# Layer 0 start and first expert tiles: where loads, statistics, products of ones and tile turns stand

## The chip, the cores and the metric

The kernel runs on one core of one Trainium2 chip. The metric is the device time of one execution in microseconds; lower is better. The kernel before took 1592.35 us, the median of three runs (1588.64, 1592.35 and 1593.25 us).

## What is computed

Two layers over 4096 tokens of width 256 (8 sequences of 512 in layer 0, 4 of 1024 for the recurrence of layer 1). Both add attention and a mixture of experts to the residual, from one layer norm:

```python
x = L0_attn_in_features
xn = _layernorm(x, axis=-1)
x = x + _L0_attn_ref(xn, ...) + _L0_ffn_ref(xn, ...)
xn = _layernorm(x, axis=-1)
x = x + _L1_attn_ref(xn, ...) + _L1_ffn_ref(xn, ...)
```

`_L0_attn_ref` is causal attention with 16 heads of 16. `_L0_ffn_ref` routes each token to 2 of 8 experts of width 512 and adds a shared network:

```python
h = _gelu(jnp.einsum('td,edf->tef', xt, Wu))
y = jnp.einsum('tef,efd->ted', h, Wd)
moe = jnp.einsum('ted,te->td', y, cw)
shared = _gelu(xt @ W1) @ W2
```

Layer 1 has a gated linear recurrence (8 heads of 32) and 8 experts of width 1024, again 2 for each token. The change touches layer 0 alone.

## The kernel before

Each engine has its own stream of instructions, written in one function for each (`sync` for SP, which issues nearly all DMAs, `gpsimd` for POOL, `scalar` for ACT, `tensor` for PE, `vector` for DVE). They meet through semaphores. The order of the attention stage is one list of steps, `attention_order()`; each engine walks it and does its part of each step. So moving a step in the list moves it on every engine that takes part in it.

A block is 512 tokens, with `x_load(b)` as its load of 512 KB. Its statistics are made by DVE for blocks 0 to 3 and by ACT for blocks 4 to 7 (`stats0`, eight passes over 256 elements). `xt` turns the normalised block with eight transposes on PE, `project(n, m)` makes queries (m = 0) or keys (m = 1) for eight heads, group n. These are cut into three bfloat16 parts: ACT takes the first, DVE the remainder and the second, POOL the third (`low_part`). SP stores the parts to DRAM (`split_out`) and, when both stores of a group are there, reads them back in another layout (`stack(n)`, 12 DMAs), from which `scores` and `scoresT` multiply. `scores` is made for the row maxima alone; the maxima go to the stacks through `maxrow(n)` (a DMA of SP), and `scoresT(n, j)` waits for them. Its exponentials are ACT's. Before the main loop a prelude handles blocks 0 and 1 and stacks 0 and 1; `ln0_steps()` spreads the normalisation of the others over the first positions of the loop.

SP's order at the start: constants, `x_load(0)`, Wq, Wk, `x_load(1)`, Wg, Wv, `x_load(2)`, `x_load(3)`; behind the store of normalised block 0 the `late_loads` (blocks 4 to 7 and Wo in four pieces); behind the 12 DMAs of `stack(0)` FW1 and the two halves of FW2, the first copies of the shared network's weights, which serve block 0 (`first_up`, `first_gelu`, `first_down`, lines 1605 and 1614) before the transposed scores begin.

At the end of layer 0's attention PE makes the shared products of blocks 1 and 2 (`HB` is 3: later blocks have theirs in the next layer), `shared_down(b, i)` with 8 matmuls each (line 1674). DVE adds their results in pairs (`shared_add`, counted by `sh_added`). Then come the experts: sorted tokens lie in 71 tiles of 128. POOL gathers a tile's rows (line 1005). For the first 8 tiles of a layer PE turns them in bank 0 of PSUM (`tile_turn`, line 1685) and DVE copies them out (line 2251). DVE also copies the expert's up weights (`weights`, line 2277). `expert_up(0, i)` writes bank 1 or 2 (line 1700), ACT takes the Gelu (line 1294), `expert_down` multiplies with Wd (line 1718). The shared products lie in banks 2 and 3. Wu and Wd (4 MB each) are loaded by SP once the attention is over; DVE waits for Wu in front of its first weights (`wu_in`), PE for Wd in front of its first down products, on line 1712. Where an expert's number is read into a register, that is a load of the engine's sequencer.

## Time and profile before

| | us |
|---|---|
| median of three runs | 1592.35 |
| profiled execution | 1598.56 |
| its span, first to last instruction | 1596.8 |
| PE busy | 1514.8 (95%) |
| DVE, ACT, POOL busy | 847.8, 746.2, 706.3 |

The profile is of one execution. Line numbers are those of the kernel before, and times on a timeline count from the span's start. PE is TensorE, PEld its weight loads, DVE VectorE, ACT ScalarE, POOL GpSimd, SP SyncE; a q behind a name is the engine's queue or sequencer. A time in brackets is idle time of the engine before the instruction, with what ended it. The clock column is the clock of TensorE that was granted, as a share of full speed (2.4 GHz; 0.50 is 1.2 GHz).

### The profile page before, as it was taken

To read this page: it belongs to the slowest core of one execution; us is meant where nothing else is said; L and a number is where in the kernel's file an instruction comes from. 1 tells how busy PE (TensorE), PEld (TensorE's weight loads), DVE (VectorE), ACT (ScalarE), POOL (GpSimd) and SP (SyncE) were. 2 spreads that over 40 slices of the span, in tenths; PEclk is the share of its full clock that TensorE was granted. 3 is DMA by queue.
4 is the path that set the end of the run, shared out by engine and by line. 5 is a ranking of instruction groups with operands and counts; after the bars stand their busy time and mean duration, and the time that the engine had idled before them with its cause. 6 is when DMAs were issued, how large, how long until landed. Compare 5 with 4: busy or idle time off the path is not lost.

```text
span 1596.8 us, 32512 instructions
## 1 busy us (share of the span) xinstructions
PE 1514.8 (95%) x10874; PEld 1168.8 (73%) x10874; DVE 847.8 (53%) x2400; ACT 746.2 (47%) x1953; POOL 706.3 (44%) x815
## 2 busy tenths in 40 slices
PE   5988989999999999999987899999999999999997
PEld 3455545555548999997664577769999999999996
DVE  4777898888713444442577988874232222223230
ACT  4665655555641323323566676545333343343432
POOL 3232326667623555553710388852333433333331
PEclk9999999999999999999998999999999999999999
DMA  8534344555215444435621489647333333333331
GB/s 266 142 114 118 98 98 83 110 111 86 68 70 201 110 114 116 111 112 147 187 94 56 123 190 177 123 79 267 56 55 54 48 59 54 57 57 54 60 54 21
DMA packets 155835, 167.60 MB, mean 105 GB/s; under 512 B 84992, under 2 KB 132988, under 8 KB 153628
## 3 DMA queue, kind: packets, MB, share of 16 engines
q1 hardware_dynamic: 131132, 128.15, 32.8%
q0 software_dynamic: 24544, 37.38, 11.0%
q8 instruction: 94, 1.54, 0.4%
q14 instruction: 65, 0.53, 0.2%
HBM read 104.10 MB, written 44.45 MB: 93 GB/s over the span
## 4 chain that ended last, share of the span: by engine, by line
PE 81%; DVE 8%; ACT 3%; issue 3%; DMA 3%; SPq 1%; POOL 0%; DVEq 0%; another core or an unknown queue 0%; ACTq 0%; POOLq 0%
PE PS L1700 23%; PE PS L1718 23%; PE PS L1557 4%; PE PS L1521 3%; PE PS L1542 3%; PE PS L1811 3%; PE PS L1493 3%; PE PS L1674 2%; DVE PS L2023 2%; PE PS L1628 2%; PE PS L1823 2%; PE PS L1583 2%; PE PS L1909 1%; PE PS L1503 1%; ACT arena L1216 1%
## 5 line engine op out<-in xcount | busy, mean ns | idle before, releaser
L1700 PEld LDWEIGHTS PS<-arena 128*128 128x128 f32 x3408 | 396.6, 192 | 11.4
L1700 PE MATMUL PS<-arena 128*128 128x128 f32 x3408 | 403.1, 275 | 0.0
L1718 PE MATMUL PS<-arena 128*128 x1704 | 392.4, 379 | 0.8 <-ACT arena L1294 0.8
L1718 PEld LDWEIGHTS PS<-arena 128*128 128x128 f32 x1704 | 311.9, 190 | 41.1 <-issue 1.2
L2023 DVE CUSTOM_DVE_ANT_0 PS<-PS,arena 128x512 f32<-128x512 f32 (+3 forms) x512 | 235.5, 523 | 48.1 <-PE PS L1521 45.1
L1019 POOL DMA_INDIRECT out<-arena x71 | 111.6, 1571 | 299.4 <-ACT arena L1312 277.6
L1302 ACT ACTIVATE arena<-PS,arena 128x128 f32<-128x128 f32 x568 | 162.3, 369 | 134.6 <-PE PS L1700 132.9
L2276 DVE COPY arena<-arena 128x8 f32 x71 | 12.4, 174 | 353.3 <-ACT arena L1302 334.7
L1312 ACT ACTIVATE arena<-PS,arena 128x256 f32<-128x256 f32 x142 | 67.4, 475 | 256.8 <-PE PS L1720 177.6
L1005 POOL DMA_INDIRECT arena<-XN,arena x142 | 144.0, 1014 | 91.9 <-issue 38.4
L1216 ACT ACTIVATE arena<-PS 128x512 f32<-128x512 f32 (+1 forms) x256 | 166.0, 704 | 32.6 <-PE PS L1542 29.2
L952 POOL TENSOR_SCALAR_AFFINE_SELECT arena<-arena 128x256 f32<-128x256 f32 x256 | 98.4, 409 | 183.2 <-ACT arena L1216 182.0
L2277 DVE COPY arena<-arena 128x1024 f32 (+1 forms) x142 | 136.4, 961 | 73.0 <-ACT arena L1294 57.5
L978 POOL DMA_INDIRECT SLOT<-arena x128 | 156.6, 1223 | 28.5 <-issue 28.2
L1012 POOL DMA_INDIRECT SUM<-arena x71 | 70.6, 994 | 96.4 <-ACT arena L1312 96.4
L1521 PE MATMUL PS<-arena 96*128 96x512 bf16 (+3 forms) x512 | 100.8, 306 | 8.8 <-DVE arena L2023 6.8
L1542 PE MATMUL PS<-arena 99*128 99x512 bf16 (+3 forms) x512 | 96.4, 302 | 7.1 <-ACT arena L1216 5.9
L1294 ACT ACTIVATE arena<-PS 128x512 f32<-128x512 f32 x71 | 42.4, 598 | 113.6 <-issue 73.9
L1542 PEld LDWEIGHTS PS<-arena 99*128 99x128 bf16 x512 | 44.4, 98 | 57.7 <-issue 17.2
L1521 PEld LDWEIGHTS PS<-arena 96*128 96x128 bf16 x512 | 48.4, 98 | 51.5 <-DVE arena L2023 16.9
L2265 DVE COPY arena<-arena 128x512 uint16<-128x512 uint16 x126 | 53.9, 428 | 60.0 <-DMA arena<-XN,arena 57.9
L1557 PE MATMUL PS<-arena 128*32 128x512 f32 (+3 forms) x1024 | 75.7, 435 | 0.5 <-issue 0.4
(248 smaller groups left out, 1993.9 us busy)
## 6 DMA issues: line engine op xcount, KB each, us to landing
arena<-FD SPq DMA_DIRECT2D x32, 512.0 KB
SPL<-arena SPq DMA_DIRECT2D x32, 384.0 KB, 3.4
arena<-SPL SPq DMA_DIRECT2D x64, 192.0 KB
XN<-arena SPq DMA_DIRECT2D x16, 512.0 KB, 3.2
arena<-SPL SPq DMA_DIRECT2D x64, 128.0 KB
arena<-SUM SPq DMA_DIRECT2D x16, 512.0 KB, 6.4
arena<-in_w SPq DMA_DIRECT2D x16, 512.0 KB
arena<-in_w SPq DMA_DIRECT2D x8, 1024.0 KB
```

The costliest lines, as they stand in the source:

```text
L978: pool.indirect_dma_start(SLOT[layer], bass.IndirectOffsetOnAxis(ap=POS[:, n, i:i + 1], axis=0), META[:, i, n, :], None).then_inc(row_out[ ...
L1005: pool.indirect_dma_start(MOE[layer].xr[i % 4][:, :], None, XN, row).then_inc(tile_in[i % 4], 16)
L1019: pool.indirect_dma_start(out, row, m.y[i % 3][:, :], None, compute_op=ALU.add).then_inc(y_out[i % 3], 16)
L1216: act.activation(PB[h % NPB][:, lo:hi], ps(3, lo, hi), ACT.Exp, scale=0.25).then_inc(p_made)
L1302: ins = act.activation(m.hT[i % len(m.hT)][:, 128 * f:128 * f + 128], ps(m.UPB[i % 2], 128 * f, 128 * f + 128), ACT.Gelu, bias=m.bias[i % ...
L1521: ins = pe.matmul(ps(0, o, o + w), q[0:96, j, 128 * i:128 * i + 128], k[0:96, j, 0:w], start=True, stop=True)
L1542: ins = pe.matmul(ps(3, o, o + w), k[0:99, j, 128 * kb:128 * kb + 128], q[0:99, j, 128 * kb:512], start=True, stop=True)
L1557: ins = pe.matmul(PS[32 * j:32 * j + 32, 6, 128 * kb:512], vb[:, kb, 8 * half + jj, :], PB[(8 * n + jj) % NPB][:, OFFT[kb]:OFFT[kb] + w], ...
L1700: ins = pe.matmul(o, m.now[i % 2][:, c * F + 128 * f:c * F + 128 * f + 128], m.xt[i % 2][:, 128 * c:128 * c + 128], start=(c == 0), stop=( ...
L1718: ins = pe.matmul(to, m.hT[i % len(m.hT)][:, 128 * c:128 * c + 128], m.WD[:, bass.ds(e * (nf * 256) + c * 256, 256)], start=(c == 0), stop ...
L2023: dve.tensor_tensor_reduce(sc, sc, MASK[:, 384 - 128 * r:512], -1.0, -NEG, ALU.add, ALU.min, NM[n % 2][:, r, j:j + 1]).then_inc(s_max)
L2277: dve.tensor_copy(m.now[i % 2][:, :], m.WU[:, bass.ds(e * m.wrow, m.wrow)]).then_inc(w_staged)
```

## The change

It has five parts, all in layer 0. (1) PE waits for the first constant and then makes 42 products of ones with ones in an unused bank, ahead of the first transposes. (2) Behind the store of normalised block 0 SP loads block 4 only. Blocks 5 to 7, FW1 and FW2 in halves and Wo follow behind `stack(0)`, in mixed order. (3) The statistics of block 5 move from the end of the prelude to the second position of the loop. (4) The semaphore of Wv and Wo is split: Wv counts with Wg, Wo has its own, and the counts of the shared weights' semaphore follow. (5) The turns of expert tiles 0 and 1 go between the last four shared down products, on PE and in DVE's order; the wait for the last shared addition moves from the front of the experts to the products of tile 1, which write a bank that the shared products use.

```diff
 def ln0_steps():
     yield []
-    yield []
+    yield [("stats", 5)]
...
-    out += [..., ("logits", 1), ("logitsT", 1), ("stats", 5)]
+    out += [..., ("logits", 1), ("logitsT", 1)]
...
-            sp.dma_start(WV[:, :, :], t["Wv"]).then_inc(wvo_in, 16)
+            sp.dma_start(WV[:, :, :], t["Wv"]).then_inc(wr_in, 16)
...
             def late_loads():
-                for b in range(4, NB):
-                    x_load(b)
+                x_load(5)
+                for k in range(2):
+                    sp.dma_start(FW1[:, k, :], t["W1"][:, k, :]).then_inc(w12_in, 16)
+                x_load(6)
+                for k in range(2):
+                    sp.dma_start(FW2[k], t["W2"][:, 2 * k:2 * k + 2, :]).then_inc(w12_in, 16)
+                x_load(7)
                 heads = t["Wo"].rearrange("(j r) g n -> j r g n", r=32)
                 for g in range(4):
                     lo = 64 * (g % 2)
-                    sp.dma_start(WO[lo:lo + 64, g // 2, :], heads[:, 0:16, g, :]).then_inc(wvo_in, 16)
+                    sp.dma_start(WO[lo:lo + 64, g // 2, :], heads[:, 0:16, g, :]).then_inc(wo_in, 16)
...
                 if kind == "norm" and a[0] < 2:
                     norm0(*a)
                     if a[0] == 0:
-                        late_loads()
+                        x_load(4)
...
                     stack(*a)
                     if a[0] == 0:
-                        sp.dma_start(FW1[:, :, :], t["W1"]).then_inc(w12_in, 16)
-                        for k in range(2):
-                            sp.dma_start(FW2[k], t["W2"][:, 2 * k:2 * k + 2, :]).then_inc(w12_in, 16)
+                        late_loads()
...
+            def spin(bk, o, many):
+                for _ in range(many):
+                    pe.matmul(ps(bk, o, o + 128), ones[:, :], ones[:, :], start=True, stop=True)
+
             def xt(b, c):
+                if b == 0 and c == 0:
+                    pe.wait_ge(const_set, 1)
+                    spin(3, 0, 42)
                 pe.wait_ge(*normed0(b))
...
             def logits(b):
                 xnt_ready(b)
-                pe.wait_ge(wr_in, 16)
+                pe.wait_ge(wr_in, 32)
...
             def project_v(b, half):
                 xnt_ready(b)
-                pe.wait_ge(wvo_in, 80)
+                pe.wait_ge(wr_in, 32)
...
             def output(b, half):
+                if b == 0:
+                    pe.wait_ge(wo_in, 64)
...
             def first_up(fc):
-                pe.wait_ge(w12_in, 48)
+                pe.wait_ge(w12_in, 64)
...
             def expert_up(layer, i):
                 pe.wait_ge(w_staged, NTILE * layer + i + 1)
+                if i == 1 and layer == 0:
+                    pe.wait_ge(sh_added, 4 * HB)
...
             def experts(layer):
                 m = MOE[layer]
-                tile_turn(layer, 0)
-                tile_turn(layer, 1)
+                if layer:
+                    tile_turn(layer, 0)
+                    tile_turn(layer, 1)
...
-            for i in range(4):
-                shared_down(HB - 1, i)
+            shared_down(HB - 1, 0)
+            tile_turn(0, 0)
+            shared_down(HB - 1, 1)
+            shared_down(HB - 1, 2)
+            tile_turn(0, 1)
+            shared_down(HB - 1, 3)
...
-            pe.wait_ge(sh_added, 4 * HB)
+            pe.wait_ge(sh_added, 4 * HB - 2)
             experts(0)
...
                 dve.wait_ge(b1_put, 1)
+                if layer == 0:
+                    dve.wait_ge(sh_gelu, 4 * HB - 4)
                 for i in range(2):
                     weights(layer, i)
                     tile_turn(layer, i)
+                    if layer == 0:
+                        shared_add(HB - 1, i)
...
-            for b in range(1, HB):
-                for half in range(2):
-                    shared_add(b, half)
-            dve.wait_ge(sh_gelu, 4 * HB - 4)
+            for half in range(2):
+                shared_add(1, half)
             experts(0)
```

## Rows read from the trace of the kernel before

**Rows 1.** The page: the chain that ended last, by engine.

```profile
PE 81%; DVE 8%; ACT 3%; issue 3%; DMA 3%; SPq 1%; POOL 0%; DVEq 0%; another core or an unknown queue 0%; ACTq 0%; POOLq 0%
```

**Rows 2.** Timeline of PE, first 75 us: start, duration, line, operation [idle before <-releaser].

```profile
12.00 1.97 PE L1464 MATMUL PS<-arena 128*128 128x128 f32 x8 [12.00 <-DVE arena L1977]
...
14.79 9.40 PE L1493 MATMUL PS<-arena 128*128 128x512 f32 x16 [0.83 <-issue]
...
34.45 1.22 PE L1521 MATMUL PS<-arena 96*128 96x512 bf16 x4 [1.74 <-DMA arena<-SPL]
...
67.87 0.72 PE L1542 MATMUL PS<-arena 99*128 99x512 bf16 x4
```

**Rows 3.** Durations (min/median/max ns) of the projections, line 1493, first 50 us.

```profile
L1493 PE MATMUL PS<-arena x24: 590/592/1194, 14.8 to 41.2; 128*128 128x512 f32 x24
```

**Rows 4.** Windows: length, busy PE, PEld, DVE, ACT, POOL, clock, DMA share, GB/s.

```profile
38.00:40.00 2.00, 2.00 (x7) 0.81 (x6) 0.24 (x1) 0.60 (x1) 0.00 (x0) 0.53 1.01 364
...
64.00:66.00 2.00, 2.00 (x14) 1.62 (x14) 1.19 (x7) 0.98 (x2) 0.64 (x1) 1.00 0.20 69
```

**Rows 5.** Timeline of PE, 460 to 512 us.

```profile
475.59 14.03 PE L1674 MATMUL PS<-arena 128*128 128x256 f32 x64
...
492.37 3.74 PE L1700 MATMUL PS<-arena 128*128 128x128 f32 x32
...
497.13 2.00 PE L1718 MATMUL PS<-arena 128*128 x8 [0.81 <-ACT arena L1294]
```

**Rows 6.** Timelines of POOL and DVE, first 50 us.

```profile
0.82 0.21 POOL L924 MEMSET arena<- 128x128 f32 x1 [0.29 <-POOLq L2558]
...
17.00 1.38 DVE L1977 TENSOR_SCALAR arena<-arena 128x256 f32<-128x256 f32 x4
...
22.66 1.09 POOL L956 TENSOR_TENSOR arena<-arena 128x512 bf16<-128x512 f32 x1 [1.05 <-DVE arena L2011]
```

**Rows 7.** Timeline of SP, first 80 us; last, the page's part 6.

```profile
21.64 2.50 SPq L714 DMA_DIRECT2D SPL<-arena  x2
...
28.21 5.56 SPq L729 DMA_DIRECT2D arena<-SPL  x12
...
44.09 5.43 SPq L729 DMA_DIRECT2D arena<-SPL  x12
...
54.74 5.43 SPq L729 DMA_DIRECT2D arena<-SPL  x12
...
61.04 0.85 SPq L738 DMA_DIRECT2D arena<-arena  x1
...
SPL<-arena SPq DMA_DIRECT2D x32, 384.0 KB, 3.4
```

**Rows 8.** Timeline of ACT, 41 to 70 us.

```profile
41.85 0.60 ACT L1189 ACTIVATE arena<-PS 128x512 bf16<-128x512 f32 x1 [2.12 <-PE PS L1493]
...
50.08 0.31 ACT L1138 ACTIVATE arena<-arena 128x16 f32<-128x16 f32 x1
...
56.28 0.60 ACT L1244 ACTIVATE arena<-PS 128x512 f32<-128x512 f32 x1 [1.67 <-PE PS L1605]
...
69.10 2.71 ACT L1216 ACTIVATE arena<-PS 128x512 f32<-128x512 f32 x4
```

**Rows 9.** Line 1712 (wait for Wd): durations, first and last start.

```profile
L1712 PEldq EVENT_SEMAPHORE  x1: 51/51/51, 495.9 to 495.9; - x1
```

**Rows 10.** Window of one us at the end of the weights' load.

```profile
495.00:496.00 1.00, 1.00 (x11) 1.00 (x11) 0.13 (x1) 0.04 (x1) 0.00 (x0) 1.00 0.17 66
```

**Rows 11.** Timeline of PE, 834 to 850 us.

```profile
838.54 3.68 PE L1811 MATMUL PS<-arena 128*128 128x512 f32 x4 [3.29 <-DVE arena L2406]
...
849.04 1.19 PE L1823 MATMUL PS<-arena 128*128 128x256 f32 x2 [3.00 <-DVE arena L2433]
```

**Rows 12.** Window of two us behind the first gap.

```profile
840.00:842.00 2.00, 2.00 (x3) 0.33 (x1) 0.00 (x0) 1.97 (x4) 0.00 (x0) 0.50 0.00 0
```

**Rows 13.** Timeline of ACT, 460 to 512 us.

```profile
494.44 0.60 ACT L1294 ACTIVATE arena<-PS 128x512 f32<-128x512 f32 x1 [18.05 <-PE PS L1700]
```

More of the change, by code:

```diff
@@ L104, in attention_order @@
     out += [("clear_meta",), ("xt0", 1), ("xt1", 1), ("project_v", 0, 0), ("project_v", 0, 1)]
-    out += [("stats", 2), ("stats", 4), ("logits", 0), ("logitsT", 0), ("stats", 3), ("logits", 1), ("logitsT", 1), ("stats", 5)]
+    out += [("stats", 2), ("stats", 4), ("logits", 0), ("logitsT", 0), ("stats", 3), ("logits", 1), ("logitsT", 1)]
     route = iter([("route", p) for p in range(20)] + [("scatter", i, (k,)) for i in range(NT) for k in range(2)])
@@ L571, in build @@
         const_set = sem("const_set")
-        wr_in, wqk_put, wqk_in, wvo_in = sem("wr_in"), sem("wqk_put"), sem("wqk_in"), sem("wvo_in")
+        wr_in, wqk_put, wqk_in, wo_in = sem("wr_in"), sem("wqk_put"), sem("wqk_in"), sem("wo_in")
         xn_out = [sem(f"xn_out{k}") for k in range(2)]
@@ L1620, in shared_up @@
                 if b == 1 and fc == 0:
-                    pe.wait_ge(w12_in, 80)
+                    pe.wait_ge(w12_in, 96)
                     pe.wait_ge(s_max, 4 * NH)
@@ L2289, in experts @@
                     halve(layer, i + 4)
-            for b in range(1, HB):
-                for half in range(2):
-                    shared_add(b, half)
-            dve.wait_ge(sh_gelu, 4 * HB - 4)
+            for half in range(2):
+                shared_add(1, half)
+            assert HB == 3
             experts(0)
```

## The prediction

> **What bounds the kernel now.** I read the page first: PE carries 81% of the chain that ended last [rows 1]. So a cut on another engine is worth something only where PE stands still, and the change touches two such places: the first 70 us, and the step from the last shared products to the first expert tiles near 490 us. Both were then read engine by engine on the timelines. The profiled execution took 1598.56 us (span 1596.8), 6.2 us over the median of the three runs, 1592.35. I make the sum as a difference against the profiled execution and put that difference on the median; 0.3%, about what a measurement of this kernel can tell from no change, is 4.8 us.
>
> At the start PE first works at 12.00 us, when block 0 is normalised [rows 2]. It works slowly there: a projection's matmul lasts 1194 ns at most and 592 ns at the median [rows 3], though the clock column has no fall that early. Sixteen of them with spacings of 0.85 or 0.43 us must fill 14.79 to 24.0 us, so about 5.6 were slow: the rate doubled near 19.6 us, 4.8 us after the projections began and 7.6 us after the first transposes. PE then runs short of work, waits for the first stack until 34.45 us, and the granted clock is at half, 1.2 instead of 2.4 GHz, from about 33 us until the end of the window from 38 to 40 us [rows 2, 4].
>
> **The products of ones.** 42 products of ones are added; a float32 product is two matmul instructions. Full rate: 32 such instructions of this shape take 3.6 us [rows 5], so 0.225 us a product; 0.45 us at half rate, by the doubling above [rows 3]. They start at 1.03 us, when POOL has set the ones [rows 6]. If the rate doubles 4.8 us later, 10.6 products are slow and 31.4 fast: 5.8 + 7.1 = 12.9 us. The trace shows no product at this place, so the bounds are the other delays it has: 3.4 us (the shortest low stretch that ended under dense work) gives 12.2 us, 7.6 us gives 14.3 us. All are behind 12.00 us: the first transposes come 0.2 to 2.3 us late, I take 0.9, since a dense stream is nearest to the projections. The eight transposes then cost about 1.0 instead of 1.97 us, so they end at 13.9 against 13.97 us. The gain comes behind them: a projection's four matmuls take 1.7 instead of 3.4 us, and DVE takes over as the bound. DVE normalises block 1 until 18.38 us [rows 6], which is hardly earlier now (18.3), and then needs 1.13 us for each projection (0.70 + 0.43). POOL's part for the second one starts at about 20.7 instead of 22.66 us [rows 6]: 1.9 us.
>
> The Trainium skill (TensorE: Matmul & The Clock Gate, "The HAM clock gate") says that the monitor behind this runs freely and is not set back by a kernel's start, so a fixed number of slow products can't be counted on. The three delays above fit that. By it the end of the 42 products would wander from run to run by some us; by my middle value it is 12.9 us.
>
> **Late loads.** Blocks 5 to 7 and Wo (1.75 MB) leave the stretch before the first splits. SP's second split store was issued near 23.8 us, 4.4 us before stack 0 could begin at 28.21 us (the two stores span 21.64 to 24.14 us); the median of this transfer is 3.4 us [rows 7]. I take 3.4: stack 0 starts at 28.21 - 1.9 - 1.0 = 25.3 us and the first scores at 31.55 instead of 34.45 us [rows 2]. The bounds are 0 and 1.5 us for the second term.
> The 1.75 MB come back behind stack 0. SP issues 11 loads there instead of 3, at some 0.46 us each (12 in 5.43 us [rows 7]), and block 1's split stores and stack 1 are queued behind them, on SP and in the DMA queues. At 364 GB/s [rows 4] they take 4.8 us. Stack 1 starts 15.9 us after stack 0 now [rows 7]; with 4.8 us more it starts at 46.0 instead of 44.09 us. Scores of stack 1 are wanted near 57 us, so that is hidden. Stack 2 follows at 56.6 instead of 54.74 us, and behind it in the same queue lies the maxima's row of the first heads, issued at 61.04 us [rows 7], whose data is through when the DMA goes quiet at about 65 us [rows 4]. That is then 66.9 us. The first transposed scores wait for this row; they start at 67.87 us now [rows 2] with about 3 us to spare, and could start at 67.0 us. Their exponentials go from 69.10 [rows 8] to about 67.8 us.
>
> **Statistics of block 5.** They move on ACT from a stretch in which ACT waits to behind the cut of projection (2,1) at 41.85 us. Two blocks' statistics fill 42.34 to 50.08 us [rows 8], 3.86 us each. Then come the roots, a table load and three Gelus, so the fourth Gelu could start 41.85 + 0.49 + 3 x 3.86 + 0.5 + 1.3 + 1.65 = 57.4 us in the old frame, against 56.28 us now [rows 8]: ACT takes 1.1 us of the 2.9 us back, and 1.8 are left before the row of maxima is asked for. Of the two limits the later counts: **1.3 us of gain at the start**, with -1.0 (products of ones until 14.3 us) and +3.0 (stack traffic hidden, low clock shorter) as bounds. Later stacks wait for PE's own scores, so this gain is kept. The split semaphores (wr_in, wo_in, w12_in) cost nothing: Wv lands with Wg, FW2 about 40 us against its first use near 43 us; if FW2 were late, PE would wait us for us.
>
> **Expert turns.** PE now ends the shared products at 489.6 us, turns tiles 0 and 1 with waits between (about 2.8 us) and starts the expert products at 492.37 us [rows 5]. With the turns in between, 4 transposes (0.4 us) and 32 products (3.6 us), with tile 2's turn, are done at about 494.0 instead of 496.2 us. DVE's first weights copy also waits for Wu, which lands at about 486 us (half of 8.4 MB from 471 us), just ahead of the second turn at 488; a wait there, with the last shared product behind it on PE, would be covered by what comes next. POOL, which gathers tile 4 once tile 0 is turned, comes to it earlier, for 0.13 MB. The wait for the shared additions moves before tile 1's products, where DVE's last addition (to about 491.0 us) is done ahead of need (491.9). The first down products wait for Wd, whose load starts at 470.8 us, at the attention's end, whatever the order of the shared products is. PE's wait for it ends at 495.9 us [rows 9], just when the DMA traffic dies away (66 GB/s in the window to 496 us [rows 10], against over 400 before); reading the expert's number takes the rest to 497.13 us [rows 5]. That wait stays where it is. So **the 2.3 us are not gained**: PE stands still from 494.0 to 497.1 us. The bounds are 0 and 3.1 us of gain (if line 1712 was passed at once and only looks like a wait).
> The new gap of 3.1 us has a price. In the next layer, PE stood still for 3.29 and 3.00 us [rows 11]; the granted clock fell at the end of both ([rows 12] is the window behind the first), for 3.4 us. The gaps of 1.05 us that this place has now did not lower it. Half speed for 3.4 us of dense expert products costs 1.7 us, and PE has no slack in the expert stage. Bounds 0 and 3.4 us (a low stretch as long as the one from 33 to 39.9 us). I take 1.7 us, as both gaps of that length fell.
>
> **Sum.** -1.3 + 1.7 = +0.4 us: profiled execution 1599.0 us, median 1592.8 us.
>
> **The rivals.**
> Forecast, chance 0.45: as summed, 1592.8 us, own range 1590.5 to 1595.
> Rival 1, the clock holds at the gap near 495 us: only the start's gain of 1.3 to 3 us is left, 1590.2 us. For it: four gaps of 1.6 to 1.8 us in the attention stage left the clock alone; against it: [rows 11]. Chance 0.27.
> Rival 2, Wd is not what PE waits for: down products start at 494.0 us. 1592.35 - 3.1 - 1.3 = 1588.0 us, and 1586.3 us with a start of 3 us. For it: the profile names ACT as releaser [rows 5]; against it: ACT's first result was there at 495.04 us [rows 13], and PE's wait ended 0.9 us later. Chance 0.13.
> Rival 3, slower: the clock stays low for two stretches behind the Wd gap (+3.4 us) and the start gains nothing, since the products of ones still run at 14 us and push everything behind the transposes. It decides from a rate doubling later than 5 us after 1.03 us. 1592.35 + 3.4 + 0.3 = 1596 us; with a start lost by 1.0 us 1597 us. Chance 0.12.
> Rest 0.03.
>
> **How the numbers follow.** Faster by over 4.8 us takes rival 2 with nearly the best start, or a gain I have not seen: 0.11. Slower by over 4.8 us takes more than the worst of rival 3: 0.05. Within: 0.84. The range reaches from rival 2 to rival 3: 1588.0 to 1596.5 us.
>
> **What would show it.** In the changed trace: products of ones ending after 12 us, and the projections at 0.43 us spacing throughout; stack 0 at about 25.3, stack 1 near 46 and stack 2 near 56.6 us; the exponentials of the first transposed scores at 67.8 us, behind a wait for DMA; PE idle from 494 to 497 us (less the start's gain), line 1712 ending where the Wd traffic ends, and the clock at half for a few us behind it. The prediction is wrong if the first down products start about 3 us earlier, or if stack 1 is not later than before: then 2 to 3 us more are gained.

## The result, and the profile after

| | before | after |
|---|---|---|
| median of six runs, us | 1593.87 | 1600.12 |
| lowest and highest | 1588.64 to 1594.95 | 1597.92 to 1602.82 |
| profiled execution | 1598.56 | 1598.96 |
| its span | 1596.8 | 1597.2 |

The change makes the kernel slower: ratio 1.0044, 95% interval 1.0028 to 1.0059, that is 7.0 us (4.5 to 9.4). The forecast was no change (1592.8 us, range 1588.0 to 1596.5). The two profiled executions differ by 0.4 us alone, and the reason lies in a stretch that the change doesn't touch: from one value projection of layer 1 (line 1823 at 906.84 us before, line 1842 at 911.54 us after) to the turn of layer 1's first expert tile (1074.28 and 1074.92 us) before took 167.4 us and after 163.4 us. Up to there after is 4.7 us later, and that is the part to be explained.

A caution for every time below that is set against a single trace of before: layer 0 of `fills_only` (further down) has the instructions of before, and its trace is 2.0 us ahead of before's at the first transposed scores (65.84 against 67.87 us) and 4.5 us ahead where the last shared products begin (465.84 against 470.39 us). So a shift of up to some 4 us between two traces need not come from a change; the gaps themselves, distances between near instructions and the timed runs are firmer.

The chain of work that ended last, by engine, has 79% PE where before had 81% [rows 1]. PE's timeline of after answers to [rows 2]; start, duration, line, operation [idle before <-releaser]. Lines are those of after: 1503 the projections, 1531 the scores, 1626 the second shared product, 1552 the transposed scores.

```profile
PE 79%; DVE 8%; DMA 4%; issue 3%; ACT 2%; SPq 2%; POOL 1%; DVEq 0%; ACTq 0%; POOLq 0%
```

```profile
1.08 12.42 PE L1464 MATMUL PS<-arena 128*128 128x128 f32 x84 [1.08 <-POOL arena L929]
...
15.20 7.11 PE L1503 MATMUL PS<-arena 128*128 128x512 f32 x16 [0.83 <-ACT arena L1171]
...
32.13 1.22 PE L1531 MATMUL PS<-arena 96*128 96x512 bf16 x4 [1.15 <-DMA arena<-SPL]
...
55.83 1.97 PE L1626 MATMUL PS<-arena 128*128 128x256 f32 x8 [1.37 <-ACT arena L1247]
...
71.08 0.72 PE L1552 MATMUL PS<-arena 99*128 99x512 bf16 x4 [4.46 <-DMA arena<-arena]
```

PE is 2.3 us ahead at the first scores (32.13 against 34.45 us) and 1.3 us ahead at 55.83 us (57.16 in before). Then it stands still for 4.46 us, for a DMA from SBUF to SBUF: the row of maxima. The first transposed scores come at 71.08 instead of 67.87 us, 3.2 us late, and the clock falls behind the gap. The other traces bear this out: 70.2 to 71.3 us behind a gap of 4.5 to 5.2 us in the four kernels with the late loads in which SP issues the row (after, `loads_only`, `wo_late`, `half_wd`), and 65.8 to 67.9 us without such a gap in the five without late loads (before, `spin_only`, `turns_only`, `turns_filled`, `fills_only`). The two groups lie 3.9 us apart on average. Windows of after (length, busy PE, PEld, DVE, ACT, POOL, clock, DMA share, GB/s), to be held against [rows 4]:

```profile
64.00:66.00 2.00, 2.00 (x15) 1.51 (x14) 1.90 (x8) 0.39 (x1) 0.46 (x1) 1.00 1.00 207
...
68.00:70.00 2.00, 0.00 (x0) 0.00 (x0) 0.00 (x0) 0.00 (x0) 0.00 (x0) 1.00 0.86 274
...
72.00:74.00 2.00, 2.00 (x10) 1.19 (x9) 1.85 (x9) 1.31 (x3) 0.77 (x2) 0.50 0.02 4
```

From 64 to 66 us the DMA moved 69 GB/s in before; now it is full, with stack 2 and what lies behind it, until about 70 us. SP's timeline answers to [rows 7]:

```profile
25.80 6.00 SPq L734 DMA_DIRECT2D arena<-SPL  x12
...
35.99 2.51 SPq L708 DMA_DIRECT2D arena<-in_Wo  x4
...
47.39 6.43 SPq L734 DMA_DIRECT2D arena<-SPL  x12
...
59.79 5.42 SPq L734 DMA_DIRECT2D arena<-SPL  x12
...
65.79 0.85 SPq L743 DMA_DIRECT2D arena<-arena  x1
```

Stack 0 starts 2.4 us earlier, stack 1 3.3 us later, stack 2 5.0 us later, and the row of maxima is issued 4.8 us later (65.79 against 61.04 us). The chain of work, followed back within the stretch, says it most plainly. First before, 34 to 68 us (shares of the chain by line):

```profile
by line: PE PS L1605 24.2%; PE PS L1614 21.7%; PE PS L1521 16.7%; DMA arena<-SPL 11.4%; PE PS L1493 10.1%; DVE PS L2023 8.3%; ACT L1216 3.8%; DVE arena L2009 3.7%; PE PS L1464 2.6%; DVE arena L2011 2.5%; issue 1.8%; ACT arena L1244 1.8%; AC
```

Then after, 36 to 72 us, with three of its pieces (start, length, what):

```profile
by line: DMA SPL<-arena 37.6%; SPq L734 30.3%; DMA arena<-arena 14.6%; issue 4.0%; PE PS L1503 2.4%; PE PS L1552 2.0%; DVE arena L2028 1.9%; ACT arena L1192 1.7%; POOL arena L959 1.2%; DVE arena L2030 1.2%; SPq L719 1.2%; SPq L712 1.2%; PE 
...
39.19 8.14 DMA SPL<-arena
...
54.33 5.41 DMA SPL<-arena
...
65.79 5.24 DMA arena<-arena
```

In before the chain ran through PE's work, and the only DMA in it was the landing of stack 0. In after it runs through stores of parts to DRAM (8.14 us for those ahead of stack 1), the issue of the stacks, and the row's own 5.24 us: this stretch has gone from PE to SP's queue. One link of this chain is misread by the profile: it hangs the stores at 39.19 us on POOL's part at 38.74 us, which belongs to the next group. The parts for stack 1 were complete at 25.45 us, and SP came to their stores at 38.55 us, behind its 12 stack reads and 11 loads.

The second place is the boundary to the experts, the answer to [rows 5], [rows 9] and [rows 10] (line 1686 the shared products, 1697 the turns, 1714 and 1732 the experts' up and down products, 1726 the wait for Wd). PE's timeline, the wait, and a window behind it:

```profile
493.91 3.73 PE L1714 MATMUL PS<-arena 128*128 128x128 f32 x32
497.48 0.38 PE L1697 MATMUL PS<-arena 128*128 128x128 f32 x2
501.81 3.67 PE L1732 MATMUL PS<-arena 128*128 x8 [3.95 <-issue]
505.32 1.95 PE L1714 MATMUL PS<-arena 128*128 128x128 f32 x16
```

```profile
L1726 PEldq EVENT_SEMAPHORE  x1: 51/51/51, 500.5 to 500.5; - x1
```

```profile
502.00:504.00 2.00, 2.00 (x5) 1.62 (x6) 0.00 (x0) 0.00 (x0) 0.00 (x0) 0.50 0.00 0
```

The shared products begin at 474.40 us here (470.39 in before), so this frame lies 4.0 us later (with the caution above). The wait ends 26.1 us behind that point, against 25.5 us in before, and the first down products come 27.41 us behind it, against 26.74. The bubbles of about 1 us in before have become one of 3.95 us, and the first eight down products take 3.67 instead of 2.0 us, at clock 0.50. The up products of tile 5 start 14.73 us behind the first down products, 13.06 us in before. This place costs 0.67 + 1.67 = 2.3 us.

### The profile page after: what moved, and what is told of

It is laid out like the page before. It is cut to its first block, busy times and chain, and to the rows that moved or that the text cites. A ratio compares the mean times of both kernels' runs of the same rounds, so it can differ in the third digit from the quotient of the medians.

```text
span 1597.2 us, 32680 instructions
## 1 busy us (share of the span) xinstructions
PE 1524.6 (95%) x10958; PEld 1178.0 (74%) x10958; DVE 852.4 (53%) x2400; ACT 747.6 (47%) x1953; POOL 714.1 (45%) x815
## 4 chain that ended last, share of the span: by engine, by line
PE 79%; DVE 8%; DMA 4%; issue 3%; ACT 2%; SPq 2%; POOL 1%; DVEq 0%; ACTq 0%; POOLq 0%
PE PS L1714 23%; PE PS L1732 23%; PE PS L1567 4%; PE PS L1552 3%; PE PS L1531 3%; PE PS L1830 3%; PE PS L1503 2%; DVE PS L2042 2%; PE PS L1595 2%; PE PS L1842 2%; PE PS L1640 2%; PE PS L1513 1%; SPq L734 1%; PE PS L1928 1%; DMA arena<-in_Wd 1%
## 5 line engine op out<-in xcount | busy, mean ns | idle before, releaser
L1015 POOL DMA_INDIRECT SUM<-arena x71 | 70.2, 988 | 104.2 <-ACT arena L1315 104.2
```

## The experiments

Each was timed beside the kernel before on the same chip (a median of 1594.1 to 1596.6 us there); ratios are against before, with the 95% interval in brackets. Where a time on a trace is given "against before", it is that of the same matmul of PE.

**The products of ones alone** (`spin_only`).

```diff
             def xt(b, c):
+                if b == 0 and c == 0:
+                    pe.wait_ge(const_set, 1)
+                    spin(3, 0, 42)
                 pe.wait_ge(*normed0(b))
```

> The kernel before with the 42 products of ones alone. Theory (the start is lost in the queue of the late loads): nothing is queued behind stack 0, the maxima's row keeps its slack, so the first transposed scores come 0 to 2 us earlier than 67.87 us and the time is 0 to 2 us below the kernel before. Rival (the products of ones cost at the start, since they end near 13.3 us and hold up the first transposes): 1 to 3 us slower than before.

Measured: 1.0006 (0.9987 to 1.0024), no difference. The products run until 13.42 us and the projections at full rate, 7.10 us for 16. POOL's part for the second projection starts at 21.38 us (22.66 in before), 1.3 us earlier. But stack 0 starts at 27.90 against 28.21 us, and the chain of this kernel shows why:

```profile
21.38 1.10 POOL arena L956
...
22.50 5.32 DMA SPL<-arena
```

The store of the parts is 1 us earlier and takes 1 us longer, among the loads of the other blocks and Wo. The gain ends in the DMA queues. In the other traces with this start and without the ones stack 0 comes at 27.59 to 27.88 us, so that even the 0.3 us may be nothing. The first transposed scores come at 66.68 us, inside the range of those traces (65.84 to 67.87 us).

**The loads and the statistics alone** (`loads_only`).

```diff
-    yield []
+    yield [("stats", 5)]
...
                     if a[0] == 0:
-                        late_loads()
+                        x_load(4)
...
                     if a[0] == 0:
-                        sp.dma_start(FW1[:, :, :], t["W1"]).then_inc(w12_in, 16)
...
+                        late_loads()
```

> The kernel before with the late loads, the split semaphores and the later statistics of block 5, without products of ones and without the turns. Theory: stack 1 starts near 48 us and stack 2 near 60 us, the first transposed scores start at 71 to 73 us behind the maxima's row, 3 to 5 us later than before: 3 to 5 us slower. Rival (ACT's third block of statistics is what delays the start): the transposed scores wait for no DMA and start at 68 to 69 us, 0 to 1 us slower.

Measured: 1.0033 (1.0015 to 1.0051), 5.3 us slower. Stack 0 starts at 25.51 us, 2.7 us earlier without any product of ones, and stacks 1 and 2 at 47.41 and 59.17 us. PE waits for the row of maxima as in after:

```profile
70.35 1.25 PE L1545 MATMUL PS<-arena 99*128 99x512 bf16 x4 [5.21 <-DMA arena<-arena]
```

The loss at the start belongs to this part.

**The row of maxima on another queue** (`max_act`): after, with the first row issued by ACT, as soon as it has it, and not by SP behind stack 2.

```diff
                 elif kind == "maxrow":
-                    maxrow(*a)
+                    if a[0]:
+                        maxrow(*a)
...
+                if n == 0:
+                    act.wait_ge(bank[bk], use + 1)
+                    act.wait_ge(s_made, 24)
+                    act.wait_ge(pads_set, 7)
+                    act.dma_start(STK[0][0][96:99, :, :], MT[0][0:24, :]).then_inc(max_in[0], 16)
```

> The changed kernel, but the maxima's row of the first eight heads is sent by ACT, in ACT's own DMA queue, instead of by SP behind stack 2 and a block's store. Theory: the gap of 4.5 us before the first transposed scores goes, they start near 66.5 us instead of 71.08, and the time is 4 to 5 us below the changed kernel, about 2 us above the kernel before. Rival (the data itself, not its place in the queue, holds the row up, or what follows is bound by stack 2): the transposed scores start at 69 us or later, at most 2 us gained.

Measured: 1.0026 (1.0008 to 1.0045). The stacks are as late as in after (47.27 and 59.23 us), and the row is issued in between:

```profile
58.76 1.33 ACTq L1213 DMA_DIRECT2D arena<-arena  x1
```

```profile
65.60 0.72 PE L1558 MATMUL PS<-arena 99*128 99x512 bf16 x4
```

The gap of 4.46 us is gone, and PE makes the first transposed scores at 65.60 us, 5.5 us ahead of after and 2.3 us ahead of before (though not ahead of `fills_only`, 65.84 us). The four traces with the row on ACT have them at 64.9 to 66.3 us. So the late row, and not the late stacks as such, cost PE its time; stacks 1 and 2 can be 3 to 4.5 us late unpunished. The time of `max_act` itself is only 2.9 us below after's ratio, less than the 4 to 5 us expected, and the intervals overlap. Clear of noise is another pair: `loads_only` (1.0033) and `max_act_no_turns` below (0.9998, 0.9983 to 1.0013) differ by the row's queue and by the ones, which bring nothing alone, and they lie 5.6 us apart. The Trainium skill (DMA: Bandwidth & Descriptors, "Queues, rings and completion order") says that SP and ACT own one row of rings each, in which a ring is consumed in order, while an engine goes round between rows by packets. The trace agrees, but doesn't test it: the row issued by ACT arrived in time although stack 2, issued 0.5 us later, kept the DMA full until 69 us, and at 58.76 us it would have stood ahead of stack 2 in SP's ring too. What the trace does show is the order of SP's instructions: ACT has made the row at 58.7 us, while SP waits for stack 2's stores until 59.23 us and then issues its 12 reads; in after the row so goes out at 65.79 us.

**Wo moved behind stack 2** (`wo_late`), otherwise as after.

```diff
                 x_load(7)
+
+            def wo_loads():
                 heads = t["Wo"].rearrange("(j r) g n -> j r g n", r=32)
...
                         late_loads()
+                    if a[0] == 2:
+                        wo_loads()
```

> The changed kernel with Wo's four loads (0.26 MB, four issues) behind stack 2 instead of behind stack 0. Theory (what is queued behind stack 0 delays stack 1, stack 2 and the maxima's row one for one): stack 1 starts 1 to 2 us earlier than 47.4 us, the first transposed scores start at 69 to 70 us instead of 71.08, 1 to 2 us below the changed kernel; but the loads behind stack 2 lie in front of the maxima's row and may take this back. Rival (the delay of the stores comes from the blocks' loads alone): stack 1 starts at the same time.

Measured: 1.0042 (1.0026 to 1.0059), as after. The queue, and the wait at its end:

```profile
24.53 5.45 SPq L736 DMA_DIRECT2D arena<-SPL  x12
...
43.91 5.44 SPq L736 DMA_DIRECT2D arena<-SPL  x12
...
61.83 2.51 SPq L710 DMA_DIRECT2D arena<-in_Wo  x4
```

```profile
70.18 1.00 PE L1556 MATMUL PS<-arena 99*128 99x512 bf16 x4 [4.49 <-DMA arena<-arena]
```

Stack 1 comes 19.4 us behind stack 0; in the seven traces with Wo ahead of it it is 21.3 to 21.9 us (21.6 in after), and in the five without late loads 14.4 to 15.9 us (15.9 in before). So Wo's 0.25 MB alone cost stack 1 some 2.2 us (1.9 to 2.5, from the one trace of `wo_late`), where its bytes at 364 GB/s [rows 4] come to 0.7 us; the rest, 3.5 to 5.0 us, goes with the 4.1 us of 1.5 MB. A rival is SP's time: Wo's four issues take 2.51 us of it, and `wo_late` comes to the stores ahead of stack 1 9.3 us behind stack 0 instead of 12.75. But the DMA is full in both until 17.6 (`wo_late`) and 18.0 us behind stack 0, so that stores issued sooner only stand in the queue longer. Wo then stands between stack 2 (issued from 55.15 us) and the row, which is issued at 64.96 us, and the gap is the same. It is a matter of what lies ahead of the row, wherever it was put.

**The turns alone** (`turns_only`).

```diff
-            for i in range(4):
-                shared_down(HB - 1, i)
+            shared_down(HB - 1, 0)
+            tile_turn(0, 0)
+            shared_down(HB - 1, 1)
+            shared_down(HB - 1, 2)
+            tile_turn(0, 1)
+            shared_down(HB - 1, 3)
```

> The kernel before with the tile turns between the last shared products alone. Theory (Wd's load gates the first down products): they start as late as before, 26.7 us after the last shared up products begin, PE stands still for 3 to 4 us in front of them, the clock falls to half behind this gap, 1 to 3 us slower than before. Rival (the turns bring their 2.3 us): first down products 2 to 3 us earlier and 2 us faster.

Measured: 1.0024 (1.0009 to 1.0039), 3.8 us slower. PE's timeline and a window:

```profile
497.24 3.77 PE L1720 MATMUL PS<-arena 128*128 x8 [3.75 <-issue]
```

```profile
500.00:502.00 2.00, 2.00 (x9) 1.82 (x8) 0.00 (x0) 0.47 (x1) 0.20 (x1) 0.50 0.00 0
```

The first up products start at 489.53 us, 2.8 us earlier than in before, and the down products at the same time (497.24 against 497.13 us). Nothing is gained, and the clock stays at half for twice as long as in after: tile 5 starts 16.03 us behind the first down products, 3.0 us more than in before. The wait for Wd itself is a little later as well. Against the begin of the shared products it ends after 26.0 to 26.3 us in the six traces with the turns and the whole of Wd, and after 24.1 to 25.8 us in the six of the old order.

**Half of Wd** (`half_wd`): after, with two of the four loads of Wd.

```diff
             for q in range(4):
-                sp.dma_start(WD0[:, 2048 * q:2048 * q + 2048], ...).then_inc(wd_in, 16)
+                if q < 2:
+                    sp.dma_start(WD0[:, 2048 * q:2048 * q + 2048], ...).then_inc(wd_in, 16)
...
+            for q in range(2):
+                pool.memset(WD0[:, 4096 + 2048 * q:6144 + 2048 * q], 0.0).then_inc(zero0)
...
-                    pe.wait_ge(wd_in, 64 + 128 * layer)
+                    pe.wait_ge(wd_in, 32 + 128 * layer)
+                    pe.wait_ge(zero0, 34)
```

> The changed kernel, but SP loads only the first two of Wd's four pieces; the other two are set to zero by POOL while PE makes the shared products. The down products of experts 4 to 7 in layer 0 so give zero: that part of the computation is left out, the instructions are the same. Theory (Wd's load is what the first down products wait for): the load ends some 5 us earlier, the gap of 4 us in front of them goes, the clock doesn't fall there, and the time is 4 to 6 us below the changed kernel. Rival (something else holds them, such as the expert's number or the first Gelu): the gap and the fall stay, same time as the changed kernel.

Measured: 1.0003 (0.9989 to 1.0018), 6.5 us below after's ratio; the intervals don't meet.

```profile
495.44 0.38 PE L1700 MATMUL PS<-arena 128*128 128x128 f32 x2
495.65 1.90 PE L1736 MATMUL PS<-arena 128*128 x8
```

Now there is no gap and no fall: the first down products start 23.29 us behind the shared products' begin, 4.1 us earlier than in after, and tile 5 12.96 us behind them. The wait for Wd is what PE waits for.

**The gap filled** (`turns_filled`): `turns_only` with 12 products of ones behind tile 2's turn.

```diff
                         tile_turn(layer, i + 2)
+                    if layer == 0 and i == 0:
+                        for _ in range(12):
+                            pe.matmul(ps(3, 0, 128), ones[:, :], ones[:, :], start=True, stop=True)
```

> The kernel before with the turns between the shared products, and 12 products of ones (2.7 us) in the gap in front of the first down products. Theory (beyond the missing gain, the loss of the turns is the clock that falls behind the gap): first down products as late as before, the clock stays at full behind them, same time as the kernel before within 1 us, 1.7 to 3.4 us below the turns alone. Rival (the turns cost through DVE's or POOL's new order): as slow as the turns alone, 1.0024 of before.

Measured: 1.0008 (0.9994 to 1.0022).

```profile
491.88 2.84 PE L1740 MATMUL PS<-arena 128*128 128x128 f32 x24
495.82 2.00 PE L1720 MATMUL PS<-arena 128*128 x8 [1.10 <-issue]
```

The down products wait as before (27.49 us behind the shared products' begin), but the clock holds, and tile 5 follows at 13.05 us. So the gap's price is the clock's fall behind it, and work without any use removes it: 3.0 us in the traces, 2.6 us between the ratios of `turns_only` and this run, whose intervals overlap. What is left is a tie with the old order: the turns have nothing to gain here, since Wd sets the time.

**The start of `max_act` with the old order at the boundary** (`max_act_no_turns`; the edits are those above).

> The changed kernel without the turns, and with the first maxima's row in ACT's DMA queue. Theory: the start is 2 to 3 us ahead of the kernel before from the first transposed scores on, and nothing takes it back: 2 to 3 us faster than before, ratio 0.998 to 0.999. Rival (a gain at the start is given back in the later stages, or the loads cost elsewhere): same as before or slower.

Measured: 0.9998 (0.9983 to 1.0013). The trace is 2.9 us ahead of before at transposed scores, 2.3 us at the last shared products, and 2.0 us at layer 1's first transposed input (768.10 against 770.10 us); the runs show none of it, though their interval reaches a gain of 2.7 us. The other traces make the lead doubtful: on average the traces with ACT's row are 1.2 us ahead of the five without late loads at the transposed scores, and `fills_only`, with before's layer 0, begins its last shared products 2.2 us sooner than this one. A gain at the start is not shown.

**Ones in layer 1's gaps** (`fills_only`): the kernel before with products of ones at three other places at the start of layer 1. In the ten traces without these fills the clock fell at the third of them each time, at the second in all but `turns_only`, and at the first in six: it held there in after (gap 2.03 us), `wo_late` (2.76), `turns_only` and `turns_filled` (1.78).

```diff
+            def ones_again(bk, many):
+                for _ in range(many):
+                    pe.matmul(ps(bk, 0, 128), ones[:, :], ones[:, :], start=True, stop=True)
+
             def project_qk(n):
                 i = ORDER1[n]
+                if n == 1:
+                    ones_again(1, 12)
...
             def project_val(n):
                 i = ORDER1[n]
+                if n == 1:
+                    ones_again(1, 11)
...
                 elif kind == "xt":
+                    if a[0] == 0:
+                        for _ in range(6):
+                            pe.matmul(ps(7, 0, 128), ones[:, :], ones[:, :], start=True, stop=True)
                     xt_next(*a)
```

> The kernel before with products of ones put on PE, at three places where it stands still at the start of layer 1: 6 ahead of the first transposed input (near 772 us, gap 2.0 us), 12 ahead of the second projection's first part (near 839 us, gap 3.3 us), 11 ahead of its value part (near 849 us, gap 3.0 us). Nothing else differs. Theory (an idle stretch of 2 us or more lowers the granted clock, and the 3.4 us at half speed behind it are lost in full where PE is the bound): the clock stays at 1.00 behind all three, and each is worth up to 1.7 us; PE is the bound behind the first alone, and behind the other two partly, so the start of the recurrence comes 1.7 to 5 us earlier than at 906.8 us, ratio 0.9985 (0.997 to 0.999). Rival (the stretches behind these gaps hang on other engines, DVE and ACT, at either clock): the clock holds, but the recurrence starts within 1 us of before, ratio 1.000.

Measured: 0.9976 (0.9961 to 0.9991), 3.8 us faster. PE's timeline of before around the first of these places and at a later one (the other two are in [rows 11]), then the same of `fills_only`:

```profile
770.10 1.77 PE L1761 MATMUL PS<-arena 128*128 128x128 f32 x8 [2.02 <-ACT arena L1354]
...
778.57 1.09 PE L1761 MATMUL PS<-arena 128*128 128x128 f32 x8
...
868.89 0.76 PE L1590 MATMUL PS<-arena 128*128 128x256 f32 x2 [1.90 <-issue]
...
899.37 1.10 PE L1823 MATMUL PS<-arena 128*128 128x256 f32 x4 [0.49 <-DVE arena L2433]
```

```profile
763.57 1.50 PE L1928 MATMUL PS<-arena 128*128 128x128 f32 x12
765.35 1.09 PE L1761 MATMUL PS<-arena 128*128 128x128 f32 x8 [0.28 <-ACT arena L1354]
...
772.15 1.09 PE L1761 MATMUL PS<-arena 128*128 128x128 f32 x8
...
832.11 1.98 PE L1817 MATMUL PS<-arena 128*128 128x512 f32 x4 [0.60 <-DVE arena L2417]
...
842.61 1.10 PE L1831 MATMUL PS<-arena 128*128 128x256 f32 x4 [0.55 <-DVE arena L2444]
...
860.87 0.67 PE L1590 MATMUL PS<-arena 128*128 128x256 f32 x2 [1.90 <-issue]
...
889.84 1.10 PE L1831 MATMUL PS<-arena 128*128 128x256 f32 x4 [0.49 <-DVE arena L2444]
```

Distances between answering rows give each gap its price against this trace of before, in which the clock fell at all of them. Behind the first, 770.10 to 778.57 is 8.47 us, and 765.35 to 772.15 is 6.80 us: 1.7 us gained. The stretches from there to the second gap last 59.97 and 59.96 us. From the second to the third (838.54 to 849.04, [rows 11]; 832.11 to 842.61) it is 10.50 us in both, though the clock was at half for 3.4 us in before and at 1.00 here: DVE sets that stretch, and the fall was free. Behind the third, 19.85 and 18.26 us: 1.6 us gained. The fourth gap, 1.90 us in both, was not filled; the clock fell behind it in before (0.57 from 869 to 873 us) and held here, for 30.48 and 28.97 us: 1.5 us more. It fell there in all ten traces without fills; with them it held in two of three and fell in `best`. Together 4.8 us, against 3.8 us by the runs (1.4 to 6.2). The theory's limit of 2 us fits neither side: a gap of 1.90 us lowered the clock and one of 2.76 us didn't.

**Both** (`best`: `max_act_no_turns` with these three fills; `best_turns`: the same with the turns and the filled gap at the boundary).

> The start of the changed kernel with the maxima's row on ACT's queue, the order at the boundary as before (no turns between the shared products), and the three fills of fills_only. Theory: the start keeps its 2.3 to 3.5 us, and the fills add 1.7 to 5 us: 4 to 8 us in the trace by the start of the recurrence, ratio 0.9975 (0.995 to 0.9985). Rival (the gains of the start are lost by the end of layer 0, or the fills bring nothing): ratio 0.9998 as without the fills.

> The same with the turns between the last shared products and 12 products of ones in the gap ahead of the first down products. Theory (the wait for Wd sets the first down products whatever stands ahead of it, and the clock holds if the gap is filled): down products start within 0.7 us of those of the kernel without turns, and the ratio is the same as that of best within 0.0015. Rival (the turns cost time of their own beyond the clock's fall): 1 us or more later than best from 510 us on.

Measured: `best` 0.9968 (0.9951 to 0.9986), `best_turns` 0.9985 (0.9971 to 1.0000). `best` is the fastest here and beats both kernels (5.1 us below before, 12 us below after by the ratios); from `fills_only` it can't be told apart. `best_turns` ends 0.0017 above it, just outside the 0.0015 expected, with intervals that overlap. Nor do its down products start within 0.7 us, as the theory had it: in the traces the first down products come 27.3 us behind the shared products' begin, against 25.8 us in `best`, and tile 5 13.05 and 12.95 us behind those. Among the kernels with the old order the first distance lay between 25.8 and 27.0 us, but for 27.3 us in `spin_only`; with the turns and the whole of Wd it lay between 27.2 and 27.5 us in all. So the rival, a cost of the turns of their own, is the better reading of the traces. No mechanism for it was shown. `spin_only` is late for a reason of its own: there the clock fell between the turns (line 1692 in that kernel), behind gaps of 1.05 us, and the 32 up products (line 1707) took 5.07 instead of 3.74 us.

```profile
491.64 0.66 PE L1692 MATMUL PS<-arena 128*128 128x128 f32 x2 [1.05 <-DVE arena L2258]
492.09 5.07 PE L1707 MATMUL PS<-arena 128*128 128x128 f32 x32
```

## Why the prediction was wrong, step by step

**The sum.** Forecast -1.3 us for the start and +1.7 us for the boundary. The traces have +2.7 us (the matmul at 92.69 us in before comes at 95.41 us) and +2.3 us. The first term has the wrong sign; the second was right in mechanism and short by 0.7 us. Both are distances in single traces. By the runs the parts alone cost 5.3 us (loads), 3.8 us (turns) and 1.0 us (ones, not distinct from nothing), and together 7.0 us; each of these is known to 2.4 to 3 us, so that 10.1 us for the parts and 7.0 us for the whole are no contradiction. The forecast for the profiled execution, 1599.0 us, met the measured 1598.96 us by luck: 4.7 us of loss stood against 4.1 us in a stretch outside the change.

**The step that failed: the time of the stacks behind the late loads.** The prediction gave stack 1 at 46.0, stack 2 at 56.6 and the row's data at 66.9 us, with 3 us to spare, and let PE ask at 67.0 us. The slack was right: in before the row was through near 65 us and nobody waited. What was put against it was too small, in four pieces. Stack 0 came at 25.80 instead of 25.3 us (0.5). Stack 1 came 21.6 us behind it instead of 20.7 (0.9), stack 2 12.4 us behind that instead of 10.65 (1.75). And PE started 1 us after the DMA had gone quiet, instead of 0.1 us (0.9). 0.5 + 0.9 + 1.75 + 0.9 = 4.1 us is the whole way from 67.0 to 71.08 us. This splits one trace; by the groups of traces above the loss is 3.9 us.

For stack 1 the best-founded piece is Wo: it cost three times its bytes (`wo_late`). In windows of half a microsecond the DMA of after has a tail:

```profile
43.50:44.00 0.50, 0.50 (x3) 0.26 (x3) 0.50 (x3) 0.41 (x3) 0.00 (x0) 1.00 0.72 246
44.00:44.50 0.50, 0.50 (x3) 0.26 (x2) 0.50 (x5) 0.50 (x3) 0.00 (x0) 0.98 0.35 119
...
45.00:45.50 0.50, 0.50 (x2) 0.15 (x1) 0.01 (x1) 0.50 (x4) 0.00 (x0) 0.50 0.34 121
```

The share stays between 0.35 and 0.27 for 2.5 us when the bulk is done, as if a third of the engines still worked, and stack 1 begins only behind that, at 47.39 us. `wo_late` has no such tail: its share is 0.07 and less from 42.5 us, and stack 1 begins at 43.91 us. Before had a tail too, of 0.13 for 1.5 us. For stack 2 the prediction took over the old distance of 10.65 us as if it were fixed. It is the shortest of all: 11.3 to 12.0 us in the other four traces without late loads and 11.2 to 12.4 us in those with them. So most of this largest piece is not the late loads' doing, but one trace's distance taken for a constant. From 50 to 56 us the DMA of after is full and moves 189 to 203 GB/s, before moved 223 to 234 GB/s in its full windows from 46 to 52 us, and `fills_only`, without late loads, 172 to 201 GB/s in its own. Why the rate differs stays open.

The bounds of the term (-1.0 to +3.0) came from the products of ones and from the clock. None came from the one quantity with a threshold: 3 us of slack, used up to 2 us by the forecast itself.

**The products of ones.** End at 13.50 us (forecast 12.9, bounds 12.2 to 14.3), projections at 0.44 us spacing, POOL's part at 21.45 instead of the forecast 20.7 us. Right in kind. In the eight traces with these products they end between 12.08 us (`best_turns`) and 13.50 us, though nothing ahead of them differs; the prediction expected such a spread. The gain of 1.9 us up to stack 0 was wrong: `spin_only` has 0.3 us, as the stores meet the loads. And the gain of the loads' absence, put at 1.0 us with 1.5 as its bound, is 2.7 us by itself. The two errors cancelled, so that stack 0 (forecast 25.3, measured 25.80 us) seemed to bear out both.

**Statistics of block 5.** ACT's fourth Gelu let PE go on at 55.83 us, 1.33 us ahead of before; the forecast left 1.8 us. Right, and without effect, as the row came last. The split semaphores cost nothing that a trace shows.

**The turns.** Up products and tile 2's turn done early, down products bound by Wd (`half_wd`), a gap of 3.95 us (forecast 3.1), the clock at half for 3.4 us behind it, 1.67 us of loss (forecast 1.7): all as put down. Missed were 0.67 us at the wait itself, which "stays where it is" by the prediction; all six traces with the turns have it later than any of the old order. The upper bound of 3.4 us was needed: `turns_only` shows 3.0 us.

**The rivals.** Rival 1 (the clock holds) fell in each of the four traces with the gap unfilled (after, `turns_only`, `max_act`, `wo_late`). What the prediction gave for it, four gaps of 1.6 to 1.8 us that left the clock alone, left out a fifth: behind the gap of 1.68 us at 86.41 us the clock of before fell to 0.50 from 88 to 91 us. Rival 2 (Wd is not the gate) fell with `half_wd`. Rival 3 came nearest in its time, and its second half, two low stretches, is in `turns_only`. Its condition at the start was met (by the prediction's working an end at 13.50 us means that the rate doubled 6 us after the ones began), but not what it said would follow: stack 0 came 2.4 us earlier, not later. The start was lost at the other end, where the row stands in SP's queue. (In other traces the ones ended sooner, at 12.9 us in `wo_late` and `half_wd`, with the same gap for the row.) That stack 1 comes later than booked and the row with it should have been the rival on the slow side.

## What to carry to other kernels

A load that is put behind a stage's transfers is not free because the bytes fit: list what is queued behind it on the same issuing queue down to the smallest transfer, and find the slack of each; a small transfer that one engine waits for is better issued by an engine that comes to it sooner. Where the next wait is set by a weight load, work brought forward only collects the idle time in one place, and one gap of 4 us lowered the clock in all four traces that have it, the gaps of 1 us in one of six. A gap that lowers the clock is worth filling with useless products, if PE is the bound behind it and the fill ends before the awaited data: 29 products at three places gave 3.8 us, while 42 at the start gave nothing. And before a distance of one trace goes into a sum, take it from several: stack 2's ranged over 1.3 us in the five traces without late loads.

## What the runs showed of the hardware

The same idle gap of 1.90 us ahead of line 1590 lowered TensorE's clock in before and left it alone in `fills_only`; at layer 1's first transposed input a gap of 2.02 us lowered it in before and one of 2.76 us left it alone in `wo_late`. Even gaps of 1.05 us were followed by a fall in `spin_only`, and by none in before. A fall lasted 3.4 us behind the gap in after and 6.8 us behind one of nearly the same length in `turns_only` (3.95 and 3.75 us). So a single trace doesn't price a gap to better than 0 to 3.4 us. The Trainium skill (TensorE: Matmul & The Clock Gate, "The HAM clock gate") calls the monitor free-running, which would let equal gaps end differently; the traces agree with that and don't prove it.

A low DMA share is no sign of a landed transfer: at a share of 0.34 stack 1 was held back for 2 us more. And 0.25 MB in four pieces of 64 KB delayed the transfers behind them by some 2.2 us (one trace of `wo_late`), about half of what 1.5 MB in large blocks did.
